# Row scores of the last sequence: sixteen pairs ahead brought back to thirteen

## The reference, cut to what matters

```
xn = layernorm(x)
q, k, v = xn Wq^T + bq, xn Wk^T + bk, xn Wv^T + bv        # 16 heads of 8
a = softmax(q k^T / sqrt(8))                              # per head, 512 x 512
x = x + (a v) Wo^T + bo
y = layernorm(x)
top 2 of 8 experts by softmax(y Wr); each expert and one shared: gelu(y Wfc + b) Wproj + b, 128 -> 512 -> 128
x = x + shared(y) + gated sum of the two chosen experts
```

## Time and profile before

| what | value |
|---|---|
| runs | 602.15, 605.17, 605.32 us |
| span of the profiled execution (first to last instruction) | 600.2 us |
| TensorE busy | 585.2 us, 98% of the span |
| VectorE busy | 497.1 us, 83% |
| ScalarE busy | 452.8 us, 75% |
| GpSimd busy | 280.1 us, 47% |
| chain that ended last | TensorE 91%, ScalarE 3% |
| row maxima, line 1002 | 256 of 1212 ns |
| exp, line 865 | 512 of 603 ns |

### The profile page before, as it was taken

How to read it: one execution, slowest core, us unless ns; L and a number is a source line. 1 busy time by engine, 2 the same in 40 slices (tenths; PEclk the granted TensorE clock), 3 DMA queues, 4 the chain that set the end, 5 groups by cost and what they waited for, 6 DMA issues and landing times.

```text
span 600.2 us, 21750 instructions
## 1 busy us (share of the span) xinstructions
PE 585.2 (98%) x8258; PEld 405.9 (68%) x8258; DVE 497.1 (83%) x1076; ACT 452.8 (75%) x967; POOL 280.1 (47%) x481
## 2 busy tenths in 40 slices
PE   6898999999999999999999999999999999999997
PEld 3443556555665655655655765656899999999966
DVE  8989999999999999999999999735577777777557
ACT  5887898888888888888888888985266555555551
POOL 7947430222542542542642642656745555555500
PEclk9999999999999999999999999999999999999999
DMA  6896333324434322322322311001422222222173
GB/s 177 224 303 208 110 80 93 102 79 121 126 91 128 90 57 61 85 57 64 82 57 66 82 56 47 21 20 49 93 56 67 70 70 70 71 70 70 42 294 136
DMA packets 43839, 57.66 MB, mean 96 GB/s; under 512 B 11130, under 2 KB 31482, under 8 KB 43754
## 3 DMA queue, kind: packets, MB, share of 16 engines
q1 hardware_dynamic: 39434, 47.59, 28.1%
q0 software_dynamic: 4320, 8.89, 4.6%
HBM read 35.76 MB, written 20.42 MB: 94 GB/s over the span
## 4 chain that ended last, share of the span: by engine, by line
PE 91%; ACT 3%; SPq 2%; DMA 1%; DVE 1%; issue 1%; POOL 0%; DVEq 0%; ACTq 0%
PE ps L1423 18%; PE ps L1451 18%; PE ps L1466 18%; PE ps L1677 11%; PE ps L1665 11%; PE ps L1624 4%; PE ps L1615 4%; PE ps L1405 2%; PE ps L1655 1%; PE ps L1486 1%; ACT xn L761 1%; PE ps L1411 1%; ACT probs L774 1%; PE ps L1497 1%; ACT probs L865 1%
## 5 line engine op out<-in xcount | busy, mean ns | idle before, releaser
L1002 DVE TENSOR_REDUCE mx<-ps 128x2 f32<-128x1024 f32 x256 | 306.2, 1212 | 20.2 <-PE ps L1423 12.2
L865 ACT ACTIVATE probs<-ps 128x512 f32<-128x512 f32 x512 | 296.8, 603 | 31.5 <-PE ps L1451 13.0
L1451 PE MATMUL ps<-q_op,k_op 128*32 128x512 bf16 x2048 | 205.0, 380 | 3.0 <-DMA q_op<-mxT 2.9
L1423 PE MATMUL ps<-k_op,q_op 96*32 96x512 bf16 x2048 | 161.0, 380 | 1.8 <-DVE mx L1002 1.3
L1466 PE MATMUL ps<-probs,v_op 128*32 128x256 f32 x2048 | 160.0, 378 | 0.0
L923 ACT ACTIVATE probs<-ps,b_cur 128x128 f32<-128x128 f32 x284 | 80.8, 368 | 59.4 <-PE ps L1665 58.6
L739 POOL DMA_INDIRECT results<-rest,row_id x71 | 71.6, 1009 | 66.5 <-DVE rest L1303 48.0
L1423 PEld LDWEIGHTS ps<-k_op,q_op 96*32 96x32 bf16 x2048 | 62.1, 97 | 52.9 <-DVE mx L1002 14.2
L1466 PEld LDWEIGHTS ps<-probs,v_op 128*32 128x32 f32 x2048 | 70.9, 109 | 38.7 <-ACT probs L865 0.2
L1451 PEld LDWEIGHTS ps<-q_op,k_op 128*32 128x32 bf16 x2048 | 64.5, 95 | 46.4 <-ACT probs L865 3.1
L630 POOL DMA_INDIRECT slots<-route_sb,slot_u x64 | 63.7, 995 | 58.0 <-ACT probs L865 49.7
(11 more groups left out here) (177 smaller groups left out, 543.0 us busy)
## 6 DMA issues: line engine op xcount, KB each, us to landing
q_op<-q_scr SPq DMA_DIRECT2D x96, 96.0 KB
k_op<-k_scr SPq DMA_DIRECT2D x96, 96.0 KB
w_sb<-in_W SPq DMA_DIRECT2D x18, 256.0 KB, 3.0
probs<-slots SPq DMA_DIRECT2D x71, 64.5 KB, 1.8
q_scr<-probs SPq DMA_DIRECT2D x8, 384.0 KB, 3.8
k_scr<-probs SPq DMA_DIRECT2D x8, 384.0 KB, 3.7
k_scr<-probs SPq DMA_DIRECT2D x8, 256.0 KB, 4.4
probs<-results SPq DMA_DIRECT2D x4, 512.0 KB, 4.8
```

Of the source, the lines that this page charges most:

```text
L865: nc.scalar.activation(probs[:, i, j, :], ps[:, BANK["key", b, hg, s], :], ACT.Exp, scale=float(D) ** -0.5).then_inc(s_exp, 1)
L1002: nc.vector.reduce_max(mx[:, slot % 2, 2 * p:2 * p + 2], ps[:, bank:bank + 2, :], AX.X).then_inc(s_max, 1)
L1423: last = nc.tensor.matmul(ps[c, BK_A + a % 4, :], q_op[hg][0:SH, j, P * i + c.start:P * i + c.stop], k_op[hg][0:SH, j, :], start=True, sto ...
L1451: last = nc.tensor.matmul(ps[c, bank, :], k_op[hg][:, j, P * i + c.start:P * i + c.stop], q_op[hg][:, j, :], start=True, stop=True)
```

## The change

Three slots of the last sequence carry no pair any more: (0,14), (1,4) and (1,10). The pairs of head groups 0 and 1 slide back accordingly, and the last three, 253, 254 and 255, stand at (2,0), (2,2) and (2,4). The transpose of the maxima of head group 3 moves from (2,7) to (2,9). Banks 2 and 3 are given to key scores from (2,10) on instead of from (2,0) on. VectorE's copy of these maxima comes one step pair later (p = 4), behind the first step of `out_norm` and no longer ahead of it.

```diff
+        LEFT_OUT = ((B - 1, 0, 14), (B - 1, 1, 4), (B - 1, 1, 10))
...
-            step = FIRST_MX_STEP if (b, hg) == (0, 0) else MX_STEP
+            step = FIRST_MX_STEP if (b, hg) in ((0, 0), (B - 1, HG - 2)) else MX_STEP
...
-                    if (s % 2 == 0 or (b, hg, s) in CATCH_UP) and row_pair < NG * PAIRS:
+                    if (s % 2 == 0 or (b, hg, s) in CATCH_UP) and (b, hg, s) not in LEFT_OUT and row_pair < NG * PAIRS:
...
-                    free = LATE_BANKS if b == B - 1 and hg >= HG - 2 else SCORE_BANKS
+                    free = LATE_BANKS if b == B - 1 and (hg == HG - 1 or hg == HG - 2 and s > FIRST_MX_STEP) else SCORE_BANKS
...
-                        if last and hg == 2 and p == 3:
+                        if last and hg == 2 and p == 4:
                             last_max_out()
```

## The result

Eleven launches of the changed kernel have a median of 606.43 us (604.14 to 608.87), eleven of the kernel before 602.7 us. The ratio is 1.0048, 95% interval 1.0032 to 1.0064: slower by 2.9 us, of which the interval allows 1.9 to 3.9. (The two medians alone lie 3.7 us apart, the two means 3.0.) The time forecast was 607.4 us at +2.2.

The account below looks back on a forecast made before the run. TensorE was taken to bound steps with row scores, ScalarE's exps the last two head groups. +2.3 (last maximum) -0.1 (port) = +2.2 us on the 605.17 median gave 607.4 us, range 603.8 to 609.6.

Parts of the forecast that it names:

- the prediction's own signs of being wrong: No idle time before y's transpose, normalisation starting before the last maximum, or attention's end moving differently from group 3's start.
- The regimes and the gain ahead of (2,0): TensorE paces steps with pairs, ScalarE those without; three fewer pairs bring (2,0) forward 1.3 us plus 0 to 0.2.
- The last row maximum, 2.3 us later, and GpSimd right behind: In group 2, VectorE's last row maximum ends at 387.6 instead of 385.28; GpSimd's split follows directly.
- GpSimd's chain with the two small corrections: From last maximum to normalisation's end 6.42 us; corrections for VectorE's multiply on the shared port total -0.1.
- The stall at (2,15) as cause: TensorE waits 2.5 us at y's transpose for GpSimd's normalisation; group 3's first exp comes 2.2 us later.
- No loss comes back in group 3, the rest shifts: ScalarE's 16 exps have no hole, so none of the 2.2 us returns; logits through the attention's end shift together.
- rival 3: The clock falls in the stall, slowing group 3's TensorE steps from 0.43 to 0.87: +5.2, 610.4 us; chance 0.07.
- the contrary row: At the span's start TensorE stood 2.74 us and the clock was still at 2.4 GHz afterwards.
- Edits called free: Maxima's transpose at (2,9), banks 2 and 3 ten steps later and the later maxima copy were to cost nothing.
- Rival 1: The transpose of y is covered after all; group 2 ends 0.4 us earlier, 604.8 us; chance 0.12.
- The bounds: Ends of the terms at group 3's first exp: +1.6 to +3.1; for the last maximum's delay alone 2.0 and 2.8.
- the list of chances: Weights of the outcomes: forecast (+1.6 to +2.9) 0.66, the three rivals 0.12, 0.15 and 0.07.

Follow-up runs that it names:

- e1: The changed kernel with the transpose of y moved from (2,15) to (3,4), logits to (3,6) and (3,8); ratio to before 0.9994.
- e6: The changed kernel with only slot (1,10) left out, so one pair stands in group 2, at (2,0); ratio to before 1.0018.
- e7: The changed kernel with only slots (1,4) and (1,10) left out, two pairs at (2,0) and (2,2); ratio to before 1.0030.
- e2: The changed kernel with GpSimd's small layernorm steps put ahead of the split of the maxima in the last sequence; ratio to before 0.9996.
- e8: The kernel before with two additional steps of 1.05 us on GpSimd behind the split in the last sequence; ratio to before 1.0046.
- e4: The changed kernel with eleven additional matmuls at (2,15), ahead of the wait for y; ratio to before 1.0031.
- e3: The changed kernel with no slot left out, last pair back at (1,14), its other edits kept; ratio to before 1.0002.
- e9: The changed kernel with layernorm steps ahead of the split, transpose of y at (3,1), logits at (3,4) and (3,6); ratio to before 1.0010.
- e12: The kernel of e9 measured once more, on another chip; ratio to before 1.0010.
- e5: The changed kernel measured again without an edit; ratio to before 1.0060.

## Why the prediction was right, and where not

The path and the size of the stall are as forecast; what comes behind the stall is not. In the profile the end of the attention has moved by 3.94 us where the start of group 3 has moved by 2.30. That is one of the prediction's own signs of being wrong, and three others point the same way: the exps of group 3 take 9.49 us and not 8, the shared expert starts 3.9 us later and not 2.2, and the clock isn't at 1.00 throughout.

1. *The regimes and the gain ahead of (2,0)*: the gain is right, the regimes are less apart than I had them (e1). 1.3 us plus 0 to 0.2 forecast, 1.39 measured; 0.4 earlier at the end of group 2 forecast, 0.52 measured.
2. *The last row maximum, 2.3 us later, and GpSimd right behind*: +2.36 (+25.57 against +23.21), and e6 and e7 place it pair by pair.
3. *GpSimd's chain with the two small corrections*: right in kind and size. The normalisation takes 2.17 us now in place of 2.44, and the multiply of VectorE at 392.30 lies beside a small step (line 562) that takes 0.37 in place of the 0.20 of its neighbours. From the end of the last maximum to the end of the normalisation it is 6.33 us against 6.42, the -0.1 of the sum. The normalisation ends 2.26 later; 2.2 was the sum.
4. *The stall at (2,15) as cause*: shown from both sides. e2 takes it away with the pairs in place, e1 moves the transpose off it, e8 makes it in the kernel before.
5. *No loss comes back in group 3, the rest shifts*: right, and more is lost. The step that was sized wrong is rival 3, the fall of the clock, to which I gave a chance of 0.07 and 3 us. It came in both profiled executions of the changed kernel and in that of e8, and cost 1.5 to 1.7 us in these three (L of 43.80 and 44.00 against the 42.32 of e4; 43.70 against the 42.01 that e8's transpose of y at +31.58 and the 10.43 give). In the launches it is less sure: the ratios 1.0031 against 1.0048 and 1.0060 point to 1.0 to 1.7 us, but their intervals overlap, and at a like mean clock the difference to before is 1.9 to 2.7 us (table above). With the fall the time is still not the 610.4 us of rival 3, since the lower clock lasted 3.4 us and not half of group 3.

   My own rows had pointed at the fall: a clock that was down 2.6 us behind the last matmul beside a stall of 2.5. I let the contrary row outweigh it, and I read that row wrongly. The windows give 1.00 for that stretch, but its eleven matmuls didn't run at full speed: their median is 586 ns, while matmuls of the same shape in e4's stall take 379 ns each. First the view of before, then that of e4:
```profile
L1382 PE MATMUL ps<-q_op,mx_parts x11: 379/586/634, 2.7 to 6.3; 128*128 128x512 bf16 x11
```
```profile
L1495 PE MATMUL ps<-q_op,id_bf x10: 379/379/379, 394.7 to 396.6; 128*128 128x512 bf16 x10
```
6. *Edits called free*: not quite, 0.36 us (e3), hidden in the changed kernel by the stall as written.
7. *Rival 1* (0.4 us won): e2, e9 and e12 have its condition, a transpose of y that doesn't wait for GpSimd. L is 0.18 us shorter in e2; its launches can't tell 0.4 us from nothing, and e9's interval leaves at most 0.25.
8. *The bounds*: the sum gives +1.6 to +3.1, the list of chances +1.6 to +2.9 for the same forecast. From the terms (2.0 to 2.8, and -0.27 to +0.15) it is +1.7 to +2.95.

That 607.4 lies only 1 us from the measured 606.43 is luck. It started from a median of three (605.17) that eleven launches put at 602.7. From there +2.2 gives 604.9, which is 1.5 us too low; a base 2.5 us too high stood in for the clock that was left out.

## What to carry to other kernels

- Before sliding work along one engine, look at what sits in order behind the wait for it on a third engine. Here three pairs of matmuls moved 2.5 us, and the price came from a layernorm on GpSimd that stood behind the same wait though it needed nothing from it.
- Where two engines arrive at a point within 0.1 us of each other, a delay of either counts nearly in full: 2.04 us put in on GpSimd gave 1.96, 0.36 us on TensorE (e3) gave 0.36.
- A stall of TensorE can cost again behind it (1.7 us behind one of 2.57 in a profile); it is to be priced with the clock.
- Check a clock column of 1.00 against the length of matmuls of a known shape before an argument rests on it.

## What the runs showed of the hardware

- Stalls of TensorE of 2.06 us (e8), 2.57 and 2.59 us (changed, e5) after dense matmuls were each followed by a stretch at 1.2 GHz (in the changed kernel from 397.9 to 401.3 us); stalls of 1.74 (e7) and 0.8 us (e6) were not, nor the one filled with matmuls (e4). The fall came 0.8 us after work had begun again, or inside the stall. These are single executions each, and no run shows what decides whether the clock falls.
- The record of the clock can miss a stretch at half speed. In e4 the clock column is at 1.00 throughout, yet between 10 and 14 us two projections take 2.07 and 1.91 us that take 1.12 and 1.02 us in before; in e1, where the same two take 2.08 and 1.91, the column is down to 0.50. Before first, then e4:
```profile
9.53 1.12 PE L1405 MATMUL ps<-xnT,wq_sb 128*128 128x512 f32 x2 [0.69 <-ACT xnT L767]
```
```profile
10.24 2.07 PE L1406 MATMUL ps<-xnT,wq_sb 128*128 128x512 f32 x2 [0.69 <-ACT xnT L768]
```
- The launches of every kernel scatter over 3 to 5 us, and part of it lies before the last sequence: (0,0) starts between 362.1 and 365.5 us in the traces of before, changed and e1 to e8. It goes with these lengths. Where these projections run slowly for a few us between 8 and 16 us of the span (changed, e1, e2, e4, e5, e8), (0,0) starts at 364.1 to 365.5; where they don't (before, e3, e6, e7), at 362.1 to 362.8. So most of the 3.07 us of lead-in between the two profiles goes with a lower clock there and not with the change (estimate: the clock column of the changed kernel has 6.8 us at 1.2 GHz in that stretch, which is at most 3.4 us lost). It isn't the whole of the scatter: among launches with a recorded clock of 0.999 and above, before still goes from 601.6 to 606.0 us, unless the record misses falls there too. Why the clock is lower in some executions stays open, as do the 20 us more on two of the chips.
